# An image tower of edges, attention and a signed layer: three stages against one unrolled software pipeline

## The reference

```python
gray  = einsum('bchw,c->bhw', x, (0.2989, 0.587, 0.114))
edges = conv3x3(gray, scharr)            # two filters, SAME padding
h = abs(edges).sum(axis=1) / 2           # (16, 256, 256)
n = layernorm(h)
Q = (n @ W_dq) @ W_uq; K = (n @ W_dkv) @ W_uk; V = (n @ W_dkv) @ W_uv
attn = softmax(causal(Q K^T / 4))        # per head
h = h + (attn V) @ W_o
out = h + layernorm(h) @ sign(weight).T
```

## Time and profile before

| | us |
|---|---|
| median of 3 runs | 499.7 |
| lowest, highest | 499.44, 503.98 |
| the profiled execution | 499.42 |
| its span, first to last instruction | 497.1 |
| mean granted TensorE clock in it | 0.935 |

### The profile page before, as it was taken

One profiled execution on the slowest core, in us unless ns is written; L12 is line 12 of the kernel. 1 busy time (PEld: TensorE's weight loads), 2 busy tenths in 40 slices (PEclk: granted clock), 3 DMA queues, 4 the chain that ended last, 5 costly groups with the idle time before them and its releaser, 6 DMA issues.

```text
span 497.1 us, 11506 instructions
## 1 busy us (share of the span) xinstructions
PE 404.2 (81%) x3780; PEld 301.0 (61%) x3780; DVE 357.1 (72%) x655; ACT 223.2 (45%) x404; POOL 94.1 (19%) x204
## 2 busy tenths in 40 slices
PE   0068867678759667899999999999999987999995
PEld 0034634446536454567777777777777755787874
DVE  2765988877795436678888888888888835676664
ACT  2034535344444341366566656655566663222231
POOL 8500322322241133111111111111111100000000
PEclk9986978878898895799999999999999999999999
DMA  4999999999996955444444444444444222333231
GB/s 151 236 241 253 244 248 267 264 258 259 259 276 178 228 157 157 135 134 142 137 144 145 150 146 136 137 142 139 141 142 145 72 87 65 113 98 123 88 107 63
DMA packets 80863, 82.09 MB, mean 165 GB/s; under 512 B 6890, under 2 KB 74698, under 8 KB 80842
## 3 DMA queue, kind: packets, MB, share of 16 engines
q1 hardware_dynamic: 80842, 81.81, 58.3%
HBM read 56.17 MB, written 25.23 MB: 164 GB/s over the span
## 4 chain that ended last, share of the span: by engine, by line
PE 49%; DMA 23%; SPq 10%; issue 7%; ACT 5%; DVE 4%; POOL 1%; ACTq 0%; DVEq 0%; POOLq 0%
DMA gray_padded<-gray 16%; PE bank L980 11%; PE bank L876 6%; PE bank L906 5%; PE bank L927 5%; PE bank L947 4%; SPq L337 3%; SPq L359 3%; PE bank L908 3%; PE bank L890 3%; PE bank L878 3%; PE bank L892 3%; PE bank L915 2%; PE bank L930 2%; PE bank L817 2%
## 5 line engine op out<-in xcount | busy, mean ns | idle before, releaser
L752 DVE TENSOR_REDUCE neg_max<-bank 128x4 f32<-128x1024 f32 x64 | 78.3, 1223 | 26.5 <-PE bank L878 26.5
L600 ACT ACTIVATE shared<-bank 128x1024 f32<-128x1024 f32 x64 | 65.6, 1025 | 70.3 <-PE bank L908 70.3
L824 PE MATMUL bank<-shared,band 128*32 128x256 f32 x512 | 44.1, 503 | 37.3 <-DMA shared<-gray_padded 37.3
L503 POOL TENSOR_TENSOR parts<-rest,parts 128x1024 bf16<-128x1024 f32 x16 | 38.5, 2404 | 133.3 <-DVE parts L727 133.3
L876 PE MATMUL bank<-k_st,q_st 96*128 96x256 bf16 x256 | 48.7, 285 | 7.5 <-DMA k_st<-qk_parts 3.3
L824 PEld LDWEIGHTS bank<-shared,band 128*32 128x32 f32 x512 | 18.8, 134 | 57.6 <-issue 46.0
L761 DVE TENSOR_TENSOR bank<-bank,cap_kq 128x512 f32<-128x512 f32 x64 | 44.2, 691 | 4.3 <-PE bank L915 4.3
L906 PE MATMUL bank<-q_st,k_st 99*128 99x256 bf16 x256 | 46.3, 274 | 0.6 <-DMA q_st<-max_rows 0.6
L927 PE MATMUL bank<-shared,v_now 128*32 128x256 f32 x512 | 42.7, 389 | 1.2 <-ACT shared L616 1.2
L756 DVE TENSOR_REDUCE neg_max<-bank 128x4 f32<-128x512 f32 x64 | 43.6, 681 | 0.0
L563 ACT ACTIVATE edge<-bank 128x512 f32<-128x512 f32 x32 | 19.1, 598 | 54.0 <-PE bank L824 53.9
(11 more groups left out here) (100 smaller groups left out, 794.3 us busy)
## 6 DMA issues: line engine op xcount, KB each, us to landing
shared<-in_x SPq DMA_DIRECT2D x16, 768.0 KB, 7.0
shared<-gray_padded SPq DMA_DIRECT2D x48, 256.0 KB
qk_parts<-parts SPq DMA_DIRECT2D x16, 768.0 KB, 6.6
q_st<-qk_parts SPq DMA_DIRECT2D x96, 128.0 KB, 2.6
k_st<-qk_parts SPq DMA_DIRECT2D x96, 128.0 KB, 2.7
gray_padded<-gray SPq DMA_DIRECT2D x16, 258.0 KB, 6.3
attn_scratch<-attn SPq DMA_DIRECT2D x16, 256.0 KB, 2.5
a_sb<-attn_scratch SPq DMA_DIRECT2D x16, 256.0 KB, 2.8
```

The lines of the kernel that those rows point to most:

```text
L503: pool.tensor_tensor(parts[:, done.slot, SLOTS_OF_PART[2], :, :], rest[:, :, :, :], parts[:, done.slot, SLOTS_OF_PART[1], :, :], ALU.subtr ...
L600: nc.scalar.activation(probs[:, g, :, 0:S], ps_k0, ACT.Exp, scale=SCALE).then_inc(exp0_done, 1)
L752: nc.vector.tensor_reduce(neg_max[:, 1, heads], ps_hi, AX.X, ALU.max, negate=True).then_inc(max_hi_done, 1)
L824: last = nc.tensor.matmul(ps_edge[b * RB:(b + 1) * RB, t, f, :], band[:, f, :], rows[:, here.slot, t * (P // RB) + b, :], start=True, stop ...
```

## The change

The three staged loops become one program, written out in full for steps -6 to 20. In step i, the scores by query are those of image i; the front part works on images i+4 (gray, rows), i+3 (filters, edges) and i+2 (norm, projections, parts), the scores by key on i-1, values on i-1 and i-2, output turn on i-2, projection on i-3, the signed layer on i-4. The cores of the diff:

```diff
-    attn_dram = nc.dram_tensor("attn_scratch", ...)
-        h_all = sb("h_all", [P, IMAGES, T, D])
-        v_all = sb("v_all", [P, IMAGES, T, D])
+        h_ring = sb("h_ring", [P, H_RING, T, D])          # H_RING = 8
+        v_ring = sb("v_ring", [P, V_RING, T, H, VW])      # V_RING = 5
+        ps_z, ps_y: bank 0; ps_edge, ps_hi: banks 0, 1; ps_lo, ps_at: bank 2
+        ps_k0, ps_qk: banks 3, 4; ps_k1, ps_mt, ps_yt: bank 5; ps_o: 6
+        ps_xt, ps_c, ps_v, ps_ot: bank 7
```

(The last three lines stand for the views of `bank` in the new code.) q and k in row halves, one weight tensor, on TensorE:

```diff
-                    for i, w in enumerate((w_q, w_k)):
-                        for t in range(T):
-                            last = nc.tensor.matmul(ps_qk[:, i, t, :],
-                                                    w[:, t, :, :].rearrange("p d h -> p (d h)"),
-                                                    c_t[:, past.slot, :], start=True, stop=True)
+            def expand_qk(n):
+                pe.wait_ge(c_copied, n + 1)
+                need(pe, exp0_done, NG * upto(n - 4) + (3 if live(n - 3) else 0))
+                need(pe, rest_done, 2 * n)
+                for t in range(T):
+                    for i, low in ((0, 0), (1, DC)):
+                        last = nc.tensor.matmul(ps_qk[:, i, t, :],
+                                                w_qk[low:low + DC, t, :, :].rearrange("p d h -> p (d h)"),
+                                                c_t[low:low + DC, :], start=True, stop=True)
+                        if t == T - 1:
+                            last.then_inc(qk_done, 1)
```

Norms on GpSimd (`normalize_y` is the same on y), in place of VectorE's L708 to L718 and ScalarE's square root:

```diff
+            def normalize_x(n):
+                pool.wait_ge(mv_done, T * (n + 1))
+                pool.tensor_scalar(var[:, :], mv[:, :, 1], EPS, None, ALU.add).then_inc(var_done, 1)
...
+                pool.tensor_tensor(rstd[:, :], var[:, :], power[:, :], ALU.pow).then_inc(rstd_done, 1)
...
+                pool.tensor_tensor(shift[:, :], mv[:, :, 0], rstd[:, :], ALU.mult).then_inc(shift_done, 1)
...
+                pool.tensor_scalar(shift[:, :], shift[:, :], -1.0, None, ALU.mult).then_inc(shift_done, 1)
...
+                for t in range(T):
+                    pool.tensor_scalar(xn[:, t, :], h_ring[:, n % H_RING, t, :], rstd[:, t:t + 1],
+                                       shift[:, t:t + 1], ALU.mult, ALU.add).then_inc(xn_done, 1)
...
+            for i in range(FIRST, LAST + 1):
+                if live(i - 1): cut_max(i - 1, 1)
+                if live(i + 2): normalize_x(i + 2)
+                if live(i - 3): normalize_y(i - 3)
+                if live(i): cut_max(i, 0)
+                if live(i + 2): third_part(i + 2)
```

More of the change, by code:

```diff
@@ L69, with live, upto, need @@
 SCALE = DK ** -0.5
[L72 to L101, removed]
+FIRST = -6
+LAST = IMAGES + 4
+H_RING = 8
+V_RING = 5
+def live(n):
+    return 0 <= n < IMAGES
+def upto(n):
+    return min(max(n + 1, 0), IMAGES)
+def need(engine, semaphore, count):
+    if count > 0:
+        engine.wait_ge(semaphore, count)
 def build(nc, x, scharr, w_dq, w_uq, w_dkv, w_uk, w_uv, w_o, w_ffn, out):
@@ L186, in build @@
[L186 to L201, removed]
+        ps_xt = bank[:, 7, :].rearrange("p (c s) -> p c s", c=T)
+        ps_c = bank[:, 7, 0:S]
+        ps_v = bank[:, 7, :].rearrange("p (t d) -> p t d", t=T)
+        ps_ot = bank[:, 7, :]
@@ L432, in _ @@
-            sp.dma_start(w_out[:, :, :], w_o.rearrange("(t p) n -> p t n", p=P)).then_inc(weights_in, 16)
-            steps(sp, front, 4, 3, first=-1, last=LAST_X)
-            sp.wait_ge(parts_out[0], 16)
-            load_operands(At(0, 0, 0), 0)
-            load_operands(At(0, 0, 0), 1)
-            for k in range(LAST_X + 1, IMAGES + 3):
-                front(k // 2, k % 2)
-            for s in range(2):
-                sp.wait_ge(parts_out[s], 16 * IMAGES // 2)
-            steps(sp, attention, 1, 2, first=0, last=IMAGES)
@@ new lines, in rest_of_parts, with max_hi @@
+            def rest_of_parts(n):
+                need(dve, part2_done, n)
+                for i in range(2):
+                    dve.wait_ge(part0_done, 2 * n + i + 1)
+                    nc.vector.tensor_tensor(rest[:, i, :, :], ps_qk[:, i, :, :], parts[:, n % 2, 4 * i, :, :],
+                                            ALU.subtract).then_inc(rest_done, 1)
+            def max_hi(n, g):
+                heads = slice(g * G, (g + 1) * G)
+                if g % 2 == 0:
+                    need(dve, cut[1], 2 * n - 1 + g // 2)
+                dve.wait_ge(hi_done, NG * n + g + 1)
+                nc.vector.tensor_reduce(neg_max[:, 1, heads], ps_hi, AX.X, ALU.max,
+                                        negate=True).then_inc(max_hi_done, 1)
@@ L802, in front_step @@
                     make_band()
-                if isinstance(j, int) and 2 * j + u == -1:
+                if i == -3:
                     make_weights()
-            steps(dve, front_step, 2, 2)
-            dve.wait_ge(drawn, 2 * TAPS + 5)
-            steps(dve, attention, 0, 2)
-            steps(dve, tail, 0, 1)
+                if live(i):
+                    max_hi(i, 1)
+                    max_lo(i, 1)
+                if live(i - 1):
+                    cap(i - 1, 1)
+                if live(i - 3):
+                    add_y(i - 3)
@@ L812, in _ @@
+                if live(i - 2):
+                    normalize(i - 2, 1)
         @block.tensor
         def _(pe):
+            two = G // 2
             def turn(dst, src, done):
@@ L863, in _, with filters @@
-            two = G // 2
-            def hi_scores(a, g):
-                at = NG * a.n + g
-                q = q_st[0:KQ, a.slot, :, :]
-                k = k_st[0:KQ, a.slot, :, :]
-                if g % 2 == 0:
-                    pe.wait_ge(st_in[a.slot][g // 2], PRODUCTS * 16 * a.turn)
-                pe.wait_ge(max_hi_done, held(at))
+                last.then_inc(done, 1)
+            def filters(n):
+                pe.wait_ge(rows_in[n % 2], ROW_LOADS * 16 * (n // 2 + 1))
+                need(pe, max_hi_done, NG * upto(n - 3))
+                need(pe, y_done, upto(n - 6))
+                need(pe, z_done, upto(n - 7))
+                need(pe, abs_done, n)
+                for t in range(T):
+                    for f in range(FILTERS):
+                        for b in range(P // RB):
+                            last = nc.tensor.matmul(ps_edge[b * RB:(b + 1) * RB, t, f, :], band[0:KC, f, :],
+                                                    rows[0:KC, n % 2, t * (P // RB) + b, :],
+                                                    start=True, stop=True)
+                    last.then_inc(filters_done, 1)
```

1075 lines of the change are left out of this document (541 added, 534 removed).

## The result

The changed kernel took 510.07 us (median of 4, 506.39 to 513.44) against 499.57 for the kernel before (median of 4, 498.42 to 503.98): a ratio of 1.0191 with a 95% interval of 1.0112 to 1.0271. It is not faster: the interval lies above 1, and on both sides of a loss of 2%. The forecast was 456 us, with a range of 436 to 492. The profiled execution took 510.3 with a span of 508.4.

The account below looks back on a forecast made before the run. TensorE was taken to bound the steady step: 22.6 us of work plus waits made 24.7. Start and steps 0 to 2 (to 108), ten full steps (247) and the ending steps reached 454, forecast 456 us, range 436 to 492.

Parts of the forecast that it names:

- Row halves: In expand_qk, q and k on separate row halves run side by side, taking 0.87 us instead of 1.73.
- Waits of the full step: TensorE's waits in a full step: about 2.0 us plus 0.2 for the port, giving a step of 24.7 us.
- `turn_x` waits for GpSimd ... Covered by 0.4: TensorE's turn of the normalized image: GpSimd ready 6.1 us into the step, needed at 6.5; 0.7 wait if slower and blocked.
- 0.5 to 0.8 of `filters`: Quarter 3 into 4: filters shares banks with max_hi 3 and waits for it, 0.5 to 0.8 us a step.
- 17 + 17 + 18: Length in us of steps 0 to 2, from each image's DMA (17.8) and operands coming 13 us behind the third part.
- Start: Before step 0: first filters at about 22 us, then one serial chain per image, first scores at 56 us.
- Step 16: 14. Step 17: 9. Last image ... 13.6: Pipeline end: step 16 without hi and lo 14 us, step 17 9 us, the last image alone 13.6 us.
- Kept on chip: Attention output without its HBM scratch: saves DMA traffic of 2 x 256 KB x 16, leaving 73.7 of 82.1 MB.
- A: Rival: waits right in place but larger (row halves in series, slower GpSimd, hops); step 27, 486 us; chance 0.18.
- B: Rival: TensorE's clock falls inside the step, mean about 0.87; slower than before at 515 us; chance 0.07.
- C: Rival: the queue absorbs the waits and the start is shorter; step 23.3, 438 us; chance 0.15.
- D: Rival: SyncE's queue order sets the step, pushing the next image's operands 3 us late; step 27.5, 484 us; chance 0.1.

Follow-up runs that it names:

- norm_first: Changed kernel with GpSimd subtracting the third part of an image one step later, behind normalize_x instead of ahead of it: 487.3 us, ratio 0.9746.
- norm_dve: Changed kernel with the two wide 128x256 steps of each normalization moved from GpSimd back to VectorE: 483.4 us, ratio 0.9633.
- warm: Changed kernel with filler matmuls, computing nothing used, in TensorE's waits of steps -1 to 3: 499.8 us, ratio 0.9969.
- fill_early: drain with filters, edges and sums of images 1 and 2 at the head of steps -2 and -1: 460.7 us, ratio 0.9226.
- fill_warm: fill_early with filler matmuls, computing nothing used, in the waits of steps 0 to 3: 461.8 us, ratio 0.921.
- drain: Changed kernel with norm_first, norm_dve, values(i-2, 2) ahead of feed_forward, and image 15 projected in step 17 ahead of image 14's turn: 467.6 us, ratio 0.9353.
- attn_hbm: Changed kernel with attention's output sent through HBM again (store, wait, load per image) before turn_attn: 550.6 us, ratio 1.0973.

## Why the prediction was wrong

- **Bound and work.** Right. TensorE's work of a full step is 22.9 against 22.6, the clock is 1.00 there, DMA 0.67; VectorE, ScalarE and GpSimd stay below.
- **Row halves.** Forecast 0.87, measured 1.06 side by side. The overlap is as forecast; the term that was off is the length of a record on half the rows. The same 0.2 is missing in v, put at 0.86 "by count". Together these are the 0.3 to 0.4 of work above the forecast.
- **Waits of the full step.** Forecast 2.0 and 0.2 for the port, measured 2.9 in the step shown (25.78 less 22.89). `feed_forward` was put at 1.1 and is 1.0. The step that failed is "`turn_x` waits for GpSimd ... Covered by 0.4": the wait is 1.2, because the wide steps were 2.02 for 0.9 beside VectorE's gray steps, the small steps 1.7 for 1.2, and the maxima 1.1 for 0.9. norm_first and norm_dve show that it is this wait. That the sum came out only 0.7 too low is luck in part: the 0.5 to 0.8 of `filters` did not appear, as it lay under the wait of `turn_x`. The forecast's own sign of being wrong, that `turn_x` on GpSimd leads the waits, came true: it ties with `feed_forward` at 5.9. The eight steps of 25.8 are 9 us over the forecast, and step 3, still at a low clock, 4.
- **"17 + 17 + 18".** The largest miss, 70 for 52 in steps 0 to 2. They were counted by DMA and by the operands' delay. In their place stands the same GpSimd chain with less other work beside it, 2.6 to 5.3 us of wait for `turn_x` in each, and the clock that fell in it. warm takes 7 us off the three steps by the clock; norm_first and norm_dve take 6 to 9 off the begin of step 3 by shortening the chain. With the chain shortened they still take 59.2 (fill_early), and with a mean clock of 0.95 on top 60.9 (fill_warm), so 7 to 9 of the 18 stay open.
- **Start.** 66 for 56. The first filters started at 25.7, not 22, the next two at 44.6 and 62.9: each of the steps -2 and -1 took 18 to 19 us, because the filters of the next image stand behind every wait of this one. fill_early takes 7.5 of the 10 back. The recorded sum is also loose: "4.4 to land" has no row (rows 6 have 6.6 for the parts; measured 4.1), and its last terms, from 44 on, add up to 54.6 and not to 56.
- **End.** "Step 16: 14. Step 17: 9. Last image ... 13.6" became 47.8. Step 16 was right (460.6 to 475.1). Step 17 took 12.5, to the product at 487.66, and the rest 20.7. The forecast took the last image as alone; the product of image 14 stands ahead of its projection, and both last products run at the lower clock:

```profile
487.66 3.78 PE L771 MATMUL bank<-w_sign,yn_t 128*128 128x256 f32 x8 [0.68 <-ACT yn_t L550]
...
492.75 1.99 PE L771 MATMUL bank<-w_out,a_t 128*128 128x256 f32 x8 [0.68 <-ACT a_t L545]
...
499.44 1.11 PE L764 MATMUL bank<-ident,yn 128*128 128x128 f32 x4 [4.69 <-POOL yn L457]
501.22 3.78 PE L771 MATMUL bank<-w_sign,yn_t 128*128 128x256 f32 x8 [0.68 <-ACT yn_t L550]
```

The edit of drain brought 2 us of the end back; how to shorten it further stays open.
- **Kept on chip.** The forecast priced it by DMA load alone. attn_hbm shows 40 us for the round trip as it was placed there.
- **Rivals.** A comes nearest: waits larger at the place that it names, GpSimd; but its step of 27 was 25.8, and it too left the ends as they were. B (clock down throughout) did not happen, though its mechanism was at work in the first steps; that its 515 lies near the measured 510 is chance. C and D did not happen: once the order on TensorE and GpSimd was mended, the step fell to 23.7 with SyncE's order as it was.

Most of the miss, 41 of 54 us, lies outside steps 3 to 12. The forecast worked out the steady step from rows and the ends by a few guesses; with six steps of lead and four of lag on sixteen images, the ends were half of the time (66.1 + 70.0 + 64.2 + 47.8 = 248 of 508 us). In the kernel before, ends are paid per stage, and each stage's steps are short, 10, 13 and 5 us. Here a step of the ends takes 12 to 25 us although it is partly empty, because its waits run through all engines. That fill_early at 460.7 comes near the forecast of 456 does not bear the forecast out: its steady step is 23.7 for 24.7, its steps 0 to 2 take 59.2 for 52.

## What to carry to other kernels

A merged pipeline pays for its fill and drain in steps that are long although partly empty: count them as serial chains with the clock that TensorE will have there, before the steady step. In an in-order queue, put the operation that the busiest engine waits for ahead of the one that only a later step needs, and put ready work in front of a matmul that takes over a bank. Work moved to an idle engine is not free when that engine then carries the loop's chain.

## What the runs showed that was not expected

- A power on two elements per row on GpSimd takes 0.72 us (1.13 and 1.14 for the first two images), where a multiplication of the same size takes 0.19.
- Matmuls that compute nothing made the changed kernel 10 us faster, where they filled waits ahead of work on the chain, and changed nothing in fill_early, where DMA is busy nearly all the time in the steps that they fill.
- The loser of a meeting of GpSimd and VectorE changed with the place of one instruction: xn took 2.02 for 1.09 in one kernel, the gray step 1.10 for 0.69 in the other. In both meetings the operation that had begun first ran at its own length (0.68 of gray, 2.14 of the third part).
- Four f32 matmuls on 64 rows take as long as eight in pairs on two row halves, 1.06 us, and longer than four on all 128 rows, 0.86.
